# FFN middle of the last two token tiles in three column parts, with each engine's last steps written out in a new order

## The reference, cut to what matters

```python
# layer 1: a linear state-space layer, then post-norm
xB = x @ B.T ; xD = x @ D.T
state = state @ A.T + xB[t]                    # a scan over 2048 steps
x = layernorm(x + layernorm(states @ C.T + xD) * gamma + beta)
# layer 2: a gated FFN in which every operand is rounded to a 4-bit grid
def fp4_linear(x, w): return q(x) @ q(w).T     # q: blocks of 16 columns,
gate, up = fp4_linear(x, w_gate), fp4_linear(x, w_up)   # scale = max|block| / 6,
h = silu(gate) * up                            # nearest of 0 .5 1 1.5 2 3 4 6
out = layernorm(x + fp4_linear(h, w_down))     # h has 704 columns
```

## Time and profile before

| | |
|---|---|
| median of 3 runs | 567.48 us (567.11 to 568.76) |
| the profiled execution's own time | 566.68 us |
| its span, first to last instruction | 564.9 us |
| PE, DVE, ACT, POOL busy | 98%, 92%, 83%, 88% |
| granted TensorE clock, mean | 0.998 |

### The profile page before, as it was taken

The page is one execution under the profiler, slowest core; times in us unless marked ns, Lnnn a source line. Parts: engine busy times, 40 slices in busy tenths (PEclk is TensorE's granted clock), DMA queues, the critical chain, the costliest instruction groups (busy, mean ns, idle before and its releaser), DMA issues.

```text
span 564.9 us, 12830 instructions
## 1 busy us (share of the span) xinstructions
PE 551.6 (98%) x3751; PEld 495.0 (88%) x3751; DVE 518.0 (92%) x1241; ACT 468.3 (83%) x1415; POOL 494.4 (88%) x674
## 2 busy tenths in 40 slices
PE   9899999999999999999999999999999999999995
PEld 7577779999999999999999999999999999999894
DVE  4896799999999999999999999999999999999973
ACT  3557867889888998988889898888989888898756
POOL 2566887999999999999999999999999999998653
PEclk9999999999999999999999999999999999999999
DMA  8951000011121111111211111121111122100001
GB/s 291 383 182 30 5 24 24 22 41 47 56 61 60 52 60 58 49 50 59 59 52 56 58 50 50 59 59 55 54 59 49 50 59 59 56 22 19 20 20 46
DMA packets 35772, 36.25 MB, mean 64 GB/s; under 512 B 6752, under 2 KB 34464, under 8 KB 34720
## 3 DMA queue, kind: packets, MB, share of 16 engines
q1 hardware_dynamic: 35744, 35.90, 20.1%
HBM read 19.50 MB, written 8.39 MB: 49 GB/s over the span
## 4 chain that ended last, share of the span: by engine, by line
PE 90%; DVE 5%; ACT 2%; issue 1%; POOL 0%; POOLq 0%; DVEq 0%; ACTq 0%
PE gu L1434 41%; PE turned L1434 18%; PE yb L1434 8%; PE turned L1517 7%; PE turned L1460 2%; PE yb L1448 1%; PE grid L1293 1%; PE turned L1541 1%; PE turned L1540 1%; PE gu L1345 1%; PE yb L1345 1%; DVE scratch L1095 1%; DVE scratch L1133 1%; PE gu L1381 1%; PE turned L1381 1%
## 5 line engine op out<-in xcount | busy, mean ns | idle before, releaser
L1434 PE MATMUL gu<-wguHi,xtHi 128*128 128x512 f32 (+1 forms) x384 | 151.3, 394 | 0.4 <-DVE xtLo L1088 0.4
L1434 PE MATMUL gu<-wguLo,xtHi 128*128 128x512 f32 (+1 forms) x384 | 143.7, 374 | 0.0
L1434 PE MATMUL gu<-wguHi,xtLo 128*128 128x512 f32 (+1 forms) x384 | 143.7, 374 | 0.0
L560 POOL TENSOR_TENSOR scratch<-scratch 128x704 f32<-128x704 f32 x63 | 90.7, 1439 | 3.2 <-DVE scratch L1109 2.6
L571 POOL TENSOR_TENSOR scratch<-scratch 128x640 f32<-128x640 f32 x64 | 81.4, 1271 | 7.6 <-DVE scratch L1133 7.4
L1434 PE MATMUL turned<-wdHi,htHi 128*128 128x256 f32 x295 | 83.7, 284 | 0.0
L1434 PE MATMUL turned<-wdHi,htLo 128*128 128x256 f32 x295 | 83.6, 283 | 0.0
L1434 PEld LDWEIGHTS gu<-wguHi,xtLo 128*128 128x128 f32 x384 | 72.2, 188 | 12.3
L1434 PE MATMUL turned<-wdLo,htHi 128*128 128x256 f32 x295 | 82.6, 280 | 0.0
L1434 PEld LDWEIGHTS gu<-wguHi,xtHi 128*128 128x128 f32 x384 | 72.2, 188 | 9.9 <-DVE xtLo L1088 1.1
L1434 PEld LDWEIGHTS gu<-wguLo,xtHi 128*128 128x128 f32 x384 | 72.4, 189 | 8.2
(11 more groups left out here) (225 smaller groups left out, 1679.7 us busy)
## 6 DMA issues: line engine op xcount, KB each, us to landing
xT<-in_L_attn_x_dram SPq DMA_DIRECT2D x8, 1024.0 KB, 9.9
scratch<-in_L_attn_x_dram SPq DMA_DIRECT2D x64, 128.0 KB, 2.4
out_dram<-scratch SPq DMA_DIRECT2D x64, 128.0 KB, 1.9
xtTile<-xT SPq DMA_DIRECT2D x48, 128.0 KB, 2.1
stTile<-statesHi SPq DMA_DIRECT2D x128, 8.0 KB, 1.7
stTile<-statesLo SPq DMA_DIRECT2D x64, 8.0 KB, 1.7
scratch<-in_L_ffn_w_down_dram SPq DMA_DIRECT2D x1, 704.0 KB, 10.3
scratch<-in_L_ffn_w_up_dram SPq DMA_DIRECT2D x1, 640.0 KB, 8.9
```

The costliest lines, as they stand in the source:

```text
L560: nc.gpsimd.tensor_tensor(blocks(hx[:, m % 2, :]), blocks(hx[:, m % 2, :]), each_block(hRc[:, m % 4, :], FB), ALU.mult).then_inc(s_xnh, 1)
L1434: ins = nc.tensor.matmul(to, l, r, start=(first and q == 0), stop=(last and q == len(passes) - 1))
```

## The change

The loop over the tiles stays as it is. For PE, ACT, DVE and POOL the passes behind the loop are no longer made by `run` but written out, in an order of their own; SP keeps its order. In them:

- Tiles 62 and 63, (7, 6) and (7, 7), go through the FFN middle in three column parts of 256, 256 and 192 columns of h, from gate and up on to the down product. An `up_part` matmul writes gate and up of the same columns, so it has 512, 512 and 384 columns as before, and reads its weights in two pieces.
- The block maxima of the parts are kept in SBUF (`hAm`), so `scale_part` is a tensor_scalar from SBUF to SBUF.
- All but one of the unread matmuls ahead of each of the last two down products are gone.
- `norm3` and `nr3` of the last two tiles are replaced by one DVE tensor_scalar, `norm_last`.
- norm3, nm3, sq3 and pow3 of the tiles before are moved ahead by up to two tiles, and sq3 writes its unused squares to `xTile` in place of `junk`.

```diff
-        SPLIT = 1
-        last_hm = [grid[:, 0:HALF], grid[:, 512:512 + FF - HALF]]
-        last_ht = [turned[:, 512:512 + HALF], turned[:, 0:HALF]]
+        SPLIT = 2
+        PARTS = ((0, 2 * P), (2 * P, 4 * P), (4 * P, FF))
+        hm_parts = [grid[:, 0:2 * P], grid[:, 512:512 + 2 * P], grid[:, 2 * P:FF - 2 * P]]
+        ht_parts = [turned[:, 512:512 + 2 * P], turned[:, 0:2 * P], turned[:, 512 + 2 * P:512 + 4 * P]]
...
-            for i in range(last):
+            for i in range(last if eng is nc.sync else 0):
                 step(HALVES, i, False)
...
+            def max_part(h, m, k):
+                dve.wait_ge(s_h, part(tile, k))
+                nc.vector.tensor_reduce(hAm[:, m % 4, bl], blocks(hx[:, m % 2, a:b]), AX_X, ALU.max, ...)
+            def scale_part(h, m, k):
+                dve.wait_ge(s_ham, part(tile, k))
+                nc.vector.tensor_scalar(hSc[:, m % 4, bl], hAm[:, m % 4, bl], SIXTH, MIN_SCALE, ALU.mult, ALU.max)
+            def norm_last(h, m):
+                dve.wait_ge(s_pow3, done(h, m))
+                nc.vector.tensor_scalar(outTile[:, r, :], x1[:, m, :], nm3t[:, m:m + 1], rs3[:, m:m + 1], ALU.add, ALU.mult)
...
+            # PE, from up_part of tile 62 on
+            up_part(7, 6, 0)
+            h_turn(7, 4)
+            up_part(7, 6, 1)
+            up_part(7, 6, 2)
+            x_turn(7, 7)
+            ffn_down(7, 4)
+            up_part(7, 7, 0)
+            h_turn(7, 5)
+            up_part(7, 7, 1)
+            up_part(7, 7, 2)
+            turn_part(7, 6, 0)
+            turn_part(7, 6, 1)
+            ffn_down(7, 5)
+            turn_part(7, 6, 2)
+            down_part(7, 6, 0)
+            down_part(7, 6, 1)
+            turn_part(7, 7, 0)
+            down_part(7, 6, 2)
+            turn_part(7, 7, 1)
+            down_part(7, 7, 0)
+            turn_part(7, 7, 2)
+            down_part(7, 7, 1)
+            down_part(7, 7, 2)
...
+            # DVE, its last steps
+            sum_part(7, 7, 1)
+            grid_part(7, 7, 1)
+            sum_part(7, 7, 2)
+            grid_part(7, 7, 2)
+            lo_part(7, 7, 0)
+            add_x1(7, 6)
+            lo_part(7, 7, 1)
+            lo_part(7, 7, 2)
+            norm_last(7, 6)
+            add_x1(7, 7)
+            norm_last(7, 7)
```

More of the change, by code:

```diff
@@ L945, in _ @@
                       (x_abs, 3), (ve1, 1), (ve3, 9)], FILLED["act"])
+            nr2(7, 5)
+            norm3(6, 5)
+            nm3(6, 7)
+            norm2(7, 5)
+            sq3(6, 7)
+            nm3(7, 0)
+            ve3(6, 7)
+            sq3(7, 0)
+            h_hi(7, 1)
+            nr3(6, 6)
+            nm2(7, 6)
+            ve3(7, 0)
+            h_abs(7, 2)
+            sq2(7, 6)
+            silu_gate(7, 3)
+            ve2(7, 6)
+            x_abs(7, 5)
+            x_hi(7, 4)
@@ new lines, in _ @@
+            nr3(6, 7)
+            nr2(7, 6)
+            mean_square(7, 7)
+            norm3(6, 6)
+            norm3(6, 7)
+            norm2(7, 6)
+            ve1(7, 7)
+            nr3(7, 0)
+            nm3(7, 1)
+            norm3(7, 0)
+            sq3(7, 1)
+            h_hi(7, 2)
+            ve3(7, 1)
+            nm2(7, 7)
+            h_abs(7, 3)
+            silu_gate(7, 4)
+            sq2(7, 7)
+            x_hi(7, 5)
+            ve2(7, 7)
+            x_abs(7, 6)
+            nr3(7, 1)
@@ new lines, in _ @@
+            norm3(7, 1)
+            nr2(7, 7)
+            norm2(7, 7)
+            nm3(7, 2)
+            sq3(7, 2)
+            ve3(7, 2)
+            h_hi(7, 3)
+            h_abs(7, 4)
+            silu_gate(7, 5)
+            nr3(7, 2)
+            norm3(7, 2)
+            x_hi(7, 6)
+            x_abs(7, 7)
+            nm3(7, 3)
+            sq3(7, 3)
+            silu_part(7, 6, 0)
+            ve3(7, 3)
+            h_hi(7, 4)
+            h_abs(7, 5)
+            silu_part(7, 6, 1)
+            nr3(7, 3)
@@ new lines, in _ @@
+            norm3(7, 3)
+            silu_part(7, 6, 2)
+            x_hi(7, 7)
+            abs_part(7, 6, 0)
+            silu_part(7, 7, 0)
+            nm3(7, 4)
+            abs_part(7, 6, 1)
+            h_hi(7, 5)
+            sq3(7, 4)
+            silu_part(7, 7, 1)
+            ve3(7, 4)
+            abs_part(7, 6, 2)
+            silu_part(7, 7, 2)
+            hi_part(7, 6, 0)
+            hi_part(7, 6, 1)
+            nr3(7, 4)
+            abs_part(7, 7, 0)
+            norm3(7, 4)
@@ L948, in _ @@
+            abs_part(7, 7, 1)
+            hi_part(7, 6, 2)
+            nm3(7, 5)
+            sq3(7, 5)
+            ve3(7, 5)
+            abs_part(7, 7, 2)
+            hi_part(7, 7, 0)
+            nr3(7, 5)
+            norm3(7, 5)
+            hi_part(7, 7, 1)
+            nm3(7, 6)
+            sq3(7, 6)
+            ve3(7, 6)
+            hi_part(7, 7, 2)
+            nm3(7, 7)
+            sq3(7, 7)
+            ve3(7, 7)
         @block.vector
@@ L1112, in h_sum @@
                 v = hx[:, m % 2, :]
[L1113 to L1125, removed]
+                dve.wait_ge(s_mh, done(h, m))
                 nc.vector.scalar_tensor_tensor(out=v, in0=hm, scalar=LEAST, in1=v, op0=ALU.max,
@@ L1136, in h_lo @@
             def h_lo(h, m):
[L1137 to L1146, removed]
+                dve.wait_ge(s_hi, done(h, m))
                 nc.vector.tensor_tensor(htLo[:, m % 2, :, :].rearrange("p c k -> p (c k)"), ht,
@@ L1528, in ffn_down @@
                         pe.wait_ge(s_r, done(h, m - 1))
[L1529 to L1536, removed]
-                    split_products(to, terms[KDA:], first=False, last=False)
-                else:
-                    split_products(to, terms, last=False)
+                pe.wait_ge(s_lo, done(h, m))
+                split_products(to, [((htHi[:, m % 2, q, :], htLo[:, m % 2, q, :]), (wdHi[:, q, :], wdLo[:, q, :]))
+                                    for q in range(NKD - 1)], last=False)
                 nc.tensor.matmul(to, htHi[:, m % 2, NKD - 1, :], wdHi[:, NKD - 1, :], start=False, stop=False)
@@ new lines, in turn_part @@
+            def turn_part(h, m, k):
+                tile = h * CHUNK + m
+                if k == 2:
+                    pe.wait_ge(s_lo, part(tile, 0))
+                elif is_split(tile - 1):
+                    pe.wait_ge(s_lo, part(tile - 1, 2 if k == 0 else 1))
+                else:
+                    pe.wait_ge(s_lo, tile)
+                pe.wait_ge(s_xlo, TILES)
+                pe.wait_ge(s_qh, part(tile, k))
+                for q in range(2):
+                    row = KD[2 * k + q]
+                    rows = hq[:, m % 2, row:row + P] if row + P <= FF else hTail[:, m % 2, :]
+                    ins = nc.tensor.transpose(ht_parts[k][:, q * P:(q + 1) * P], rows, ident[:, :])
+                ins.then_inc(s_t, 1)
```

301 lines of the change are left out of this document (239 added, 62 removed).

## The result

The changed kernel takes 563.41 us in the median of 9 runs (562.27 to 566.38), the kernel before 567.11 in the 9 runs beside it. The ratio is 0.9941 with a 95% interval of 0.9926 to 0.9957: 3.3 us faster, between 2.4 and 4.2. Run again beside other kernels it gave 0.9934 (0.9917 to 0.9951). The prediction was 563.3 us and 4.2 us won.

The account below looks back on a forecast made before the run. PE was taken as full until 545.57, the last 13 us as bound by the latency of whole-tile steps. Tail 3.5 + end 0.7 = 4.2 us won, 567.48 - 4.2 = 563.3 us, range 562.0 to 564.6.

Parts of the forecast that it names:

- The stretch before the tail: Reordered steps up to tile 63's first up part: taken as 0, between 0.2 us won and 1.0 lost.
- The cost of the parts: DVE passes of tiles 62 and 63: 5.6 us a tile against 4.5 uncut; weights read in two pieces cost 0.
- The wait that the parts bring: Six scale_part and norm_last on DVE may wait for POOL's running instruction: 0.6 us in all, ends 0 and 2.5.
- The tail step by step: From tile 63's up parts to its add_x1, which starts at 555.6 for 559.11: 3.5 us won.
- the walk: Going through the four new engine lists by hand, each step starting when engine and inputs are free, with the trace's durations.
- The end: Behind tile 63's add_x1: norm_last starts 2.3 us later and takes 0.3 (between 0.20 and 0.42); 0.7 us won.
- The clock rival: In the tail TensorE's clock falls to 1.2 GHz, 7.5 us of PE work take 15; time 569.4 us; chance 0.04.
- The rival in which DVE pays more: DVE, full from 540.5 to 550, takes all upper prices; gain 2.0 us, time 565.5 us; chance 0.20.
- The rival of the single chain: In the last steps each part waits for the one before; only norm_last's 0.7 us is won, 566.8 us; chance 0.07.

Follow-up runs that it names:

- the banks apart: Changed kernel with own PSUM banks for the last two down products and no unread matmuls; ratios to the kernel before 0.9911 and 0.9930.
- the doubled maxima: Changed kernel with each of six max_part done twice; from tile 62's first layer-1 matmul to the end 53.66 us for 52.30.

## Why the prediction was right, point by point

**The stretch before the tail.** Right. Tile 62's first up part starts at 536.00 (534.02, predicted 533.94), tile 63's at 542.95 (540.97, predicted 540.78; the earlier trace rows 540.95). gu0 of tile 61 was put back, as walked (528.63, shifted 526.65, before 526.39), and by tile 63 it came out at nothing.

**The cost of the parts.** Right in the sum: DVE is busy 9.48 of 9.50 us from 542.5 to 552, the stretch that was predicted full, and idle for 2.8 us from 537.9 to add_x1 of tile 63, for 2.6 predicted. One step of the working is slightly off: by its own prices a pass in three parts takes 0.33 + 0.33 + 0.27 = 0.93 and not 0.95, 0.2 us over both tiles. Up parts of 512 columns step at 0.23 us (542.95 to 544.35 for six), so that weights are read in two pieces costs nothing.

**The wait that the parts bring.** Right, with its size. The six scale_part last 0.54, 0.18, 0.31, 0.16, 0.16, 0.16 us, 0.55 above six of the shortest, for 0.6 predicted. The two long ones end at 540.61 and 545.29, and POOL's instructions at 540.58 and 545.26. By the rule of the Trainium skill (SBUF — State Buffer, Who interferes with whom) the trace agrees on DVE's side. That POOL too stood behind DVE is not seen: its parts of 256 columns last 0.62, as in the earlier trace rows.

**The tail step by step.** Right up to down of tile 62, and further: turns at 545.97 in the shifted time for 545.95, down of 61 at 546.38 for 546.4, down of 62 with its unread matmul at 549.30 for 549.3, and add_x1 of tile 62 ends at 554.59 (552.61) for 552.6. Behind that it falls back by 0.37: ACT's last hi_part ends at 556.54 (554.56) for 554.2, the last lo_part at 557.00 (555.02) for 554.7, and add_x1 of tile 63 starts at 557.95 (555.97) for 555.6. So the loss lies between the end of add_x1 and the last turn. There stand 0.15 us until the unread matmul starts at 554.74, 0.22 for that matmul, and 0.20 in place of 0.12 from the first down matmul to the second at 555.16. The term that was missing is this unread matmul: the change left one in, and the walk has none. That it is the larger part of the 0.37 is read from the rows; with it out and the banks apart, 0.5 us was won. What the walk allowed for PE's restart is not written out in the prediction, so the rest can't be parted further.

**The end.** norm_last starts 2.37 behind add_x1, for 2.3, and lasts 0.41, for 0.3: it is at its upper bound, so a tensor_scalar of 256 columns with two scalar pointers took as long as the add of the earlier trace rows. 0.55 won for 0.7. With 0.37 and 0.15 less the sum 4.2 becomes 3.68, which is M's; the timed runs have 3.3 and 3.7.

**What the prediction had by luck.** It booked the whole 3.5 us to cutting, gave the new order no price of its own, took the unread matmuls for mere filling, and walked the tail without them. The runs show M as a product, not a sum:

| M, us | old order, norm3 | new order, norm_last |
|---|---|---|
| whole tiles (in the old order tile 63 in halves), five groups unread | 55.98 (before) | 57.27 |
| whole tiles, none unread | 56.37 | 58.95 |
| three parts, five groups unread (four in the new order) | 56.51 | 55.43 |
| three parts, one unread for each of the last two down products | 55.77 | 52.30 |

The right column has norm_last in it: with norm3 its last number is 52.79. From before, none of the three wins by itself (57.27 by the order, 56.51 by the parts, 56.37 without unread matmuls). Of two together, parts with almost nothing unread win 0.2, parts in the new order 0.55, which is norm_last's, and the order with nothing unread loses 3.0. All three win 3.7. The order lets parts of two tiles pass each other on DVE, and PE's gaps become so small that the clock holds with almost nothing unread in them. Only that frees the 3.1 us that such matmuls would cost on the new chain. The walk contained all three, so its sum held; a cut priced from its parts would not have.

**The rivals.** The clock rival did not come true in this kernel, but it is real: three of its relatives, in which PE idles 1.4 to 2.4 us at a time, fell to 1.2 GHz before their last products. I gave it 0.04 and named the right mark, the gaps, which are under 0.5 us here. The rival in which DVE pays more had the right engine (the doubled maxima show it), at prices that did not occur. The rival of the single chain, with norm_last's gain alone left, came true in relatives as well: the parts in the old order, without norm_last, win 0.2, and the changed kernel with unread matmuls is left with norm_last's 0.5.

## What to carry to other kernels

Cutting the last tiles paid here only with every engine's queue rewritten for it: in succession the parts wait for each other as the whole did, and a step moved back for one engine can block another's (ACT's sq3 here). Matmuls that keep the clock up are free while they fill idle time and cost their full length when the idle time is gone; whether they can go is a question of the gaps that are left, to be read from the granted clock. A stretch measured from the last unchanged instruction to the end agreed within 0.06 us in two profiles of the same kernel, twice, and so tells half a microsecond from none, where the interval of the timed runs is some 2 us wide.

## What the runs showed of the hardware

The granted clock fell from 1.00 to 0.50 without any single PE idle time over 2.0 us: idle 1.57, a turn of 0.85, idle 1.97 did it in the kernel before without its unread matmuls. With the order alone it held behind 1.44, a turn of 0.87 and 1.97, and fell behind a second such group (1.63, 0.87, 1.97). The first down matmul behind a wait, behind transposes or behind an unread one was followed by the second 0.20 to 0.22 us later and not 0.12 (554.96 to 555.16, 555.89 to 556.10, 557.06 to 557.28), so the wait is not what makes it. A tensor_scalar of 16 or 12 columns took 0.16 to 0.18 us, and 0.54 and 0.31 where it had to end behind a running POOL instruction (0.03 us behind it both times). And two executions of the same code differed by 2 us in their first 510, with a mean clock of 0.99 in the stretch from 60 to 300 us of the later one.
